# A graph network on one core: the numbers that address PSUM banks, packed four to a word and loaded every 88 steps

## The chip, the cores and the metric

The kernel runs on one NeuronCore of one Trainium2 chip. The metric is the device time of one execution in microseconds (us), lower is better. It stands at a median of 2926.83 us over three runs, from 2922.68 to 2935.74. "PE" is TensorE, "DVE" VectorE, "ACT" ScalarE, "POOL" GpSimd and "SP" SyncE. Each engine has a sequencer of its own: it reads the engine's program, keeps registers, computes addresses in them and hands matmuls on to the array. What PE's sequencer does itself is marked PEldq in the trace.

## What is computed

Four graph layers run over 3125 nodes with 512 features and 53125 edges. The edge list is sorted by the target node. Each layer adds its result to x:

```python
h = jnp.maximum(_layernorm(x, axis=-1), 0.0)
x = x + _L0_gnn_ref(h, L0_gnn_W, src, dst, edge_weight)   # relu(segment_sum(w * (h @ W)[src], dst))
h = jnp.maximum(_layernorm(x, axis=-1), 0.0)
x = x + _L1_gnn_ref(h, edge_index, L1_gnn_W, L1_gnn_b)    # sum normalised by degrees
h = jnp.maximum(_layernorm(x, axis=-1), 0.0)
x = x + _L2_gnn_ref(h, edge_index, ...)                   # sum of neighbours, two products
h = jnp.maximum(_layernorm(x, axis=-1), 0.0)
x = x + _L3_gnn_ref(h, edge_index, Ws, Wb, a_w, a_b)      # attention with 8 heads, softmax over a node's edges
```

## The kernel before

The nodes are cut into 25 tiles of 125 (`TILES`, `TN`), the sorted edges into 416 chunks of 128 (`CHUNKS`, `CE`). A chunk may hold edges of two tiles or more, so the edges are walked in `STEPS` = 416 + 25 - 1 = 440 steps; each step belongs to one tile, and which one depends on the data. DVE computes the tile of each step near the start, PE turns the four columns of it into a row in PSUM bank 3 (L1876), and DVE copies that row to `tile_row` (L757), one 32-bit number for a step.

Three stages of PE's program walk the 440 steps and need the tile's number as an address:

- **The first layer** (`step(0, i)`, from 120 us to 793 us). POOL gathers 128 rows of 2 KB for a step into a ring of 11 slots (L2258), DVE writes a selection matrix (L1104), and PE adds selection times rows into one of three PSUM banks, chosen by the tile's number (L1841, an fp32 product that runs as two passes). The sequencer does for each step: copy the number to a fresh register (L1821), wait for the selection and for the gathered rows, mask the number and add a constant (L1837, two operations), wait for the bank to be fresh, compute the bank's address (L1841, FUSED_REGOPS). Between the steps stand projections (L1807), transposes (L1796) and counts of degrees (L1883).
- **The target stage** (`target_steps`, from 2056 us to 2309 us). The last layer's scores of targets and sources are spread over the edges. PE alternates between `source_product`, six matmuls for a pair of steps (L2156), and two small matmuls, one for each step, whose moving operand `t3[:, t]` is addressed by the tile's number (L2140). For each of these the sequencer copies the number (L1821), masks it (L2140, ALU_OP) and computes the address (L2140, FUSED_REGOPS). DVE reduces each pair's result (L1432), which frees its bank (`u_sum`).
- **The last layer** (`step(LAST, i)`, from 2357 us to the end). As the first, but DVE scales the gathered rows (L1583, `scaled`), and a second small product adds the denominators (L1845) with one more address computed.

Every 20 steps `load_tiles` (L1818) loads the next 20 numbers of `tile_row` from SBUF into 20 registers (`reg_load`, TENSOR_LOAD in the trace): 22 loads in each stage, 66 in all. Another table, `group_row`, is loaded the same way 27 times between 799 and 1140 us (L1957) for other steps.

```python
def load_tiles(i):
    P.reg_load(tile_regs, tile_row[0:1, bass.ds(i, LOADED_TILES)])

def step_tile(r):
    return nc.s_assert_within(P.snap(tile_regs[r % LOADED_TILES]) & 31, 0, TILES - 1, ...)
```

The tables are announced by the semaphore `tables`, which reaches 6 when `src_t`, `dl_t`, `w_t`, `tile_row`, `end_row` and `tid_row` are written (L754 to L766). PE opens the banks then (L1890), POOL begins to gather once the last product rows are stored too, and SP reloads x.

## Time and profile before

| | |
|---|---|
| median of 3 runs | 2926.83 us (2922.68 to 2935.74) |
| profiled execution, its own time | 2952.38 us |
| its span | 2951.1 us |
| PE busy | 2508.8 us (85%) |
| DVE busy | 1854.8 us (63%) |
| POOL busy | 872.3 us (30%) |
| ACT busy | 568.5 us (19%) |
| mean granted clock of TensorE | 0.933 |

The profiled execution took 2952.38 us, 25.55 us more than the median, so differences are worked out inside it and then taken to the median. Of its own time all but 1.3 us lies in the span. A busy share is an average over stages with different limits: what a change in one stage is worth is read from that stage. "issue" as a releaser means that the engine waited for nothing that the profile can name, which for PE includes its own sequencer.

### The profile page before, as it was taken

What the parts mean: (1) busy time and instruction counts of PE and PEld (TensorE: products, weight loads), DVE (VectorE), ACT (ScalarE), POOL (GpSimd) and SP (SyncE); (2) the same over time, 40 slices, a digit from 0 to 9 for tenths busy, and PEclk for the clock granted to TensorE, in tenths of its full rate; (3) what the DMA queues carried; (4) which work ended last, traced back from release to release, by engine and by line L of the source; (5) the groups of instructions that cost most, each with busy time, mean ns of one, the idle gap of its engine ahead of it and who ended that gap; (6) DMA issues with size and microseconds to landing.
All of it is one profiled execution on the core that took longest, in us unless ns stands there. A gap on an engine that the chain in (4) does not pass through costs nothing.

```text
span 2951.1 us, 39280 instructions
## 1 busy us (share of the span) xinstructions
PE 2508.8 (85%) x10397; PEld 1450.1 (49%) x10397; DVE 1854.8 (63%) x4953; ACT 568.5 (19%) x946; POOL 872.3 (30%) x900
## 2 busy tenths in 40 slices
PE   7888988877887777999989999997898588888777
PEld 5534443433444444666555555664787433333332
DVE  7765667586588885657333443334786387776666
ACT  4533310000055553000000000001555100000000
POOL 0366666666400000000000000000002466666665
PEclk9899999898888888999999999998999699999999
DMA  6686655666422112334711121112644466676665
GB/s 164 178 241 175 181 166 167 172 168 179 117 75 86 54 54 65 94 110 112 200 43 57 57 57 54 53 32 61 152 120 138 125 193 202 204 230 189 192 189 167
DMA packets 152926, 389.06 MB, mean 132 GB/s; under 512 B 40735, under 2 KB 42136, under 8 KB 152737
## 3 DMA queue, kind: packets, MB, share of 16 engines
q0 software_dynamic: 71040, 232.25, 27.6%
q1 hardware_dynamic: 81014, 153.03, 18.4%
q8 instruction: 117, 1.92, 0.3%
q10 hardware_dynamic: 683, 1.28, 0.2%
q14 instruction: 72, 0.59, 0.1%
HBM read 333.73 MB, written 52.72 MB: 131 GB/s over the span
## 4 chain that ended last, share of the span: by engine, by line
PE 53%; DVE 23%; issue 10%; DMA 7%; another core or an unknown queue 3%; POOL 2%; ACT 1%; SPq 1%; ACTq 0%; DVEq 0%
PE banks L1841 17%; PE banks L1979 15%; PE banks L1807 7%; DVE spare L1031 4%; PE banks L2156 4%; DVE spare L1030 3%; DMA ring<-edge_counts 3%; PE banks L1971 3%; DMA ring<-table,src_t 2%; POOL ring L2313 2%; DVE sel L1104 2%; PE banks L1796 1%; DVE ring L1583 1%; DVE rstd L884 1%
## 5 line engine op out<-in xcount | busy, mean ns | idle before, releaser
L1841 PE MATMUL banks<-ring,sel 128*125 128x512 f32 x1682 | 891.4, 658 | 160.5 <-issue 116.1
L1841 PEld LDWEIGHTS banks<-ring,sel 128*125 128x125 f32 x1682 | 287.0, 199 | 476.7 <-issue 473.4
L2258 POOL DMA_INDIRECT ring<-table,src_t x440 | 436.8, 993 | 250.5 <-issue 107.7
L2292 POOL DMA_INDIRECT x<-table,src_t x25 | 25.1, 1005 | 1493.1 <-DMA x<-src_digits 1478.4
L2313 POOL DMA_INDIRECT ring<-table,src_t x401 | 386.5, 964 | 227.9 <-PE banks L1845 98.4
L1979 PE MATMUL banks<-acc,ring 125*125 125x512 f16 x1900 | 437.9, 381 | 7.0 <-issue 7.0
L1971 PE MATMUL banks<-spare 128*125 128x325 f16 x1080 | 276.0, 370 | 73.2 <-DVE spare L1031 24.2
L1979 PEld LDWEIGHTS banks<-acc,ring 125*125 125x125 f16 x1900 | 256.9, 137 | 160.4 <-issue 27.2
L1583 DVE TENSOR_TENSOR ring<-ring,banks 128x512 f32<-128x512 f32 x388 | 255.7, 682 | 122.3 <-DMA ring<-table,src_t 99.2
L1971 PEld LDWEIGHTS banks<-spare 128*125 128x125 f16 x1080 | 152.2, 147 | 197.2 <-issue 194.7
L1031 DVE TENSOR_SCALAR spare<-node_scores,flags 128x650 f16<-128x650 f16 x540 | 207.7, 385 | 0.0
L2156 PE MATMUL banks<-bias_bc,spare 123*128 123x224 bf16 x1320 | 165.3, 268 | 28.3 <-issue 15.2
L1807 PE MATMUL banks<-wh,hTh 128*125 128x512 f32 x300 | 137.0, 457 | 58.7 <-DVE hTl L900 22.4
L1030 DVE TENSOR_SCALAR spare<-node_scores,den 128x125 f16<-128x125 f16 x540 | 138.7, 257 | 62.1 <-PE banks L1971 56.8
L1432 DVE TENSOR_REDUCE big<-banks 128x16 f32<-128x448 f32 x220 | 131.4, 618 | 69.6 <-PE banks L2156 57.5
L1979 PE MATMUL banks<-acc,sel 125*125 125x512 f16 x600 | 140.6, 379 | 0.0
L1104 DVE TENSOR_SCALAR sel<-node_iota,dl_t,w_t 128x125 f32<-128x125 f32 x440 | 136.2, 358 | 1.4 <-issue 0.4
L2156 PEld LDWEIGHTS banks<-bias_bc,spare 123*128 123x128 bf16 x1320 | 119.0, 101 | 35.0 <-issue 27.0
L1807 PE MATMUL banks<-wh,hTl 128*125 128x512 f32 x300 | 126.6, 422 | 0.0
L1807 PE MATMUL banks<-wl,hTh 128*125 128x512 f32 x300 | 126.5, 422 | 0.0
L1663 ACT CAST big<-banks 125x650 f16<-125x650 f32 x125 | 90.5, 724 | 173.7 <-PE banks L1971 173.5
L1681 ACT ACTIVATE spare<-banks 125x512 f32<-125x512 f32 x25 | 14.9, 597 | 564.0 <-PE banks L1979 564.0
(408 smaller groups left out, 2970.9 us busy)
## 6 DMA issues: line engine op xcount, KB each, us to landing
ring<-edge_counts SPq DMA_DIRECT2D x38, 683.6 KB
edge_counts<-big SPq DMA_DIRECT2D x25, 683.6 KB
ring<-table,src_t POOLq DMA_INDIRECT x841
sel<-edge_counts SPq DMA_DIRECT2D x12, 683.6 KB
acc<-dst_places SPq DMA_DIRECT2D x28, 256.0 KB
x<-dst_places SPq DMA_DIRECT2D x27, 256.0 KB
acc<-src_digits SPq DMA_DIRECT2D x28, 224.0 KB
x<-src_digits SPq DMA_DIRECT2D x27, 224.0 KB
```

Source lines behind the costliest of these rows:

```text
L1030: V.tensor_scalar(out=low_hot[j % HOTS], in0=low_names, scalar1=low_t[:, j:j + 1], scalar2=None, op0=ALU.is_equal).then_inc(hot_ok, 1)
L1031: V.tensor_scalar(out=key_hot[j % HOTS], in0=key_names, scalar1=key_t[:, j:j + 1], scalar2=None, op0=ALU.is_equal).then_inc(hot_ok, 1)
L1104: V.tensor_scalar(out=sel[:, i % SELS, :], in0=node_iota[:, :], scalar1=dl_t[:, i:i + 1], scalar2=w_t[:, i:i + 1], op0=ALU.is_equal, op1=A ...
L1432: V.tensor_reduce(ue[:, pair_step(n):pair_step(n) + 2, :], bank[2 + n % 4][:, 0:2 * CTH].rearrange("p (i t h) -> p i h t", i=2, h=H), axis ...
L1583: V.tensor_tensor(slot, slot, weights[:, :, None].to_broadcast([CE, H, DP]), ALU.mult).then_inc(scaled, 1)
L1807: last = P.matmul(to, a[:, q, k, :], b[:, k, :], start=(k == 0 and n == 0), stop=(k == KB - 1 and n == 2))
L1841: last = P.matmul(to, sel[:, n % SELS, :], rows, start=False, stop=True, skip_group_check=True)
L1971: last = P.matmul(to, low_hot[j % HOTS], key_hot[j % HOTS][:, h * HALF_W:(h + 1) * HALF_W], start=False, stop=True, skip_group_check=True)
L1979: last = P.matmul(to[0:TN, :], counts_at(n, s), acc16[0:TN, s, half * D:(half + 1) * D], start=(s == half == 0), stop=(s == TILES - 1 and ...
L2156: last = P.matmul(bank[2 + n % 4][:, i * CTH:(i + 1) * CTH], sp_hot[k % 3][0:SK, j * CE:(j + 1) * CE], u3[0:SK, part, :], start=(part == 0 ...
L2258: G.indirect_dma_start(out=ring[:, i % RING, :], out_offset=None, in_=table[0][:, :], in_offset=bass.IndirectOffsetOnAxis(ap=src_t[:, i:i ...
L2313: G.indirect_dma_start(out=rows_at(i), out_offset=None, in_=table[1][:, :], in_offset=bass.IndirectOffsetOnAxis(ap=src_t[:, i:i + 1], axis ...
```

## The change

Four tile numbers of 5 bits are packed into one word. DVE makes the words by three multiplications by 32 and three additions on one partition, 110 numbers each, in place of the copy of 440. A load now fills 22 registers, which serve 88 steps, so a stage has 5 loads. A step takes its number by a shift and a mask, and one step of four (the lowest 5 bits) by the mask alone. The group table's loads stay as they were.

```diff
-    LOADED_TILES = 20
+    GROUP_STEPS = 20
+    PACKED, PACK_BITS = 4, 5
+    LOADED_WORDS = 22
+    LOADED_STEPS = PACKED * LOADED_WORDS
...
-        tile_row = sb("tile_row", [1, STEPS], I32)
+        tile_words = sb("tile_words", [1, STEPS // PACKED], I32)
+        tile_sum = sb("tile_sum", [1, STEPS // PACKED])
...
-                V.tensor_copy(tile_row[:, :], bank[3][0:1, 0:STEPS]).then_inc(tables, 1)
+                of_step = bank[3][0:1, 0:STEPS].rearrange("p (w n) -> p w n", n=PACKED)
+                for n in range(PACKED - 1, 0, -1):
+                    high = of_step[:, :, n] if n == PACKED - 1 else tile_sum[:, :]
+                    own.mark(V.tensor_scalar(out=tile_sum[:, :], in0=high, scalar1=float(1 << PACK_BITS), scalar2=None, op0=ALU.mult))
+                    V.wait_ge(v_own, own.n)
+                    own.mark(V.tensor_tensor(tile_sum[:, :], tile_sum[:, :], of_step[:, :, n - 1], ALU.add))
+                    V.wait_ge(v_own, own.n)
+                V.tensor_copy(tile_words[:, :], tile_sum[:, :]).then_inc(tables, 1)
...
-            tile_regs = [P.alloc_register(f"tile{n}") for n in range(LOADED_TILES)]
+            tile_regs = [P.alloc_register(f"tile{n}") for n in range(LOADED_WORDS)]
...
-                P.reg_load(tile_regs, tile_row[0:1, bass.ds(i, LOADED_TILES)])
-
-            def step_tile(r):
-                return nc.s_assert_within(P.snap(tile_regs[r % LOADED_TILES]) & 31, 0, TILES - 1,
+                P.reg_load(tile_regs, tile_words[0:1, i // PACKED:i // PACKED + LOADED_WORDS])
+
+            def step_tile(i):
+                word = P.snap(tile_regs[i // PACKED % LOADED_WORDS])
+                at = i % PACKED * PACK_BITS
+                return nc.s_assert_within((word >> at if at else word) & 31, 0, TILES - 1,
...
-                if i % LOADED_TILES == 0:
+                if i % LOADED_STEPS == 0:
                     load_tiles(i)
                 t = step_tile(i)
```

The condition on `LOADED_STEPS` stands in `step` and in `target_steps`. Over the whole program PE has 42 TENSOR_LOADs in place of 93 (27 of each are the group table's), 660 more REGISTER_ALUs in the two layers, and in the target stage 330 register copies have become fused register operations.

PE's program in the target stage, around a load (L1818 or, after, L1829 is the load; L2140 or L2153 the small product and its address). Register copies are not listed. Before:

```order
L2156 MATMUL banks<-bias_bc,spare 128x224 x6
L1818 TENSOR_LOAD tile_row
L2140 REGISTER_ALU
L2140 ISA
L2140 MATMUL banks<-stage,spare 128x24
L2140 REGISTER_ALU
L2140 ISA
L2140 MATMUL banks<-stage,spare 128x24
L2156 MATMUL banks<-bias_bc,spare 128x224 x6
```

And with the change:

```order
L1829 TENSOR_LOAD tile_words
L2153 REGISTER_ALU
L2153 ISA
L2153 MATMUL banks<-stage,spare 128x24
L2169 MATMUL banks<-bias_bc,spare 128x224 x6
L1832 ISA
L2153 REGISTER_ALU
L2153 ISA
L2153 MATMUL banks<-stage,spare 128x24
L1832 ISA
L2153 REGISTER_ALU
L2153 ISA
L2153 MATMUL banks<-stage,spare 128x24
```

The ISA at L1832 is the copy and the shift in one fused operation; it stands where a register copy stood (L1821), in three steps of four.

PE's program in the last layer, around a load. Before:

```order
L1818 TENSOR_LOAD tile_row
L1837 REGISTER_ALU x2
L1841 ISA
L1841 MATMUL banks<-ring,sel 125x512
L1845 ISA
L1845 MATMUL banks<-stage,sel 125x24
L1837 REGISTER_ALU x2
L1841 ISA
L1841 MATMUL banks<-ring,sel 125x512
```

And with the change:

```order
L1829 TENSOR_LOAD tile_words
L1850 REGISTER_ALU x2
L1854 ISA
L1854 MATMUL banks<-ring,sel 125x512
L1858 ISA
L1858 MATMUL banks<-stage,sel 125x24
L1850 REGISTER_ALU x3
L1854 ISA
L1854 MATMUL banks<-ring,sel 125x512
```

Here the shift is a third ALU operation. It stands behind the wait for the step's data, since that wait is held by the first of the ALU operations.

DVE's program where the tables are written, with the change (before, one CAST of 1x440 to `tile_row` stood in place of the middle seven):

```order
L760 COPY w_t<-banks 128x440
L764 TENSOR_SCALAR tile_sum<-banks 1x110
L766 TENSOR_TENSOR tile_sum<-tile_sum,banks 1x110
L764 TENSOR_SCALAR tile_sum<-tile_sum 1x110
L766 TENSOR_TENSOR tile_sum<-tile_sum,banks 1x110
L764 TENSOR_SCALAR tile_sum<-tile_sum 1x110
L766 TENSOR_TENSOR tile_sum<-tile_sum,banks 1x110
L768 CAST tile_words<-tile_sum 1x110
L769 TENSOR_SCALAR past<-acc 1x25
```

Six operations more stand ahead of `past`, `end_row` and `tid_row`, and each waits for the one before it.

## Rows read from the trace of the kernel before

**Rows 1.** The page: busy time, and the chain that ended last.
```profile
PE 2508.8 (85%) x10397; PEld 1450.1 (49%) x10397; DVE 1854.8 (63%) x4953; ACT 568.5 (19%) x946; POOL 872.3 (30%) x900
...
PE 53%; DVE 23%; issue 10%; DMA 7%; another core or an unknown queue 3%; POOL 2%; ACT 1%; SPq 1%; ACTq 0%; DVEq 0%
```

**Rows 2.** Line L1818, whole span, then 2067:2272: count, duration min/median/max in ns.
```profile
L1818 PEldq TENSOR_LOAD <-tile_row x66: 5/1360/1648, 117.8 to 2912.7; - x66
...
L1818 PEldq TENSOR_LOAD <-tile_row x21: 1355/1360/1372, 2071.1 to 2271.6; - x21
```

**Rows 3.** PE's waits, 2067:2272: waited for, us in total, times, longest.
```profile
PE banks L2140 <- issue: 16.9, 18, 1.5
PE banks L2156 <- DVE big L1432: 1.5, 4, 0.5
```

**Rows 4.** Busy time by window, 2067:2272; DVE's waits there.
```profile
2067.00:2272.00 205.00, 184.83 (x1785) 169.25 (x1781) 163.30 (x290) 125.33 (x117) 5.44 (x5) 0.96 0.49 131
...
DVE big L1432 <- PE banks L2156: 39.8, 46, 3.2
```

**Rows 5.** PE's timeline in the target stage: start, duration, operation, idle before.
```profile
2091.90 0.29 PE L2140 MATMUL banks<-stage,spare 126*128 x2
...
2095.76 0.22 PE L2140 MATMUL banks<-stage,spare 126*128 x2
...
2098.93 0.18 PE L2140 MATMUL banks<-stage,spare 126*128 x1
2100.54 0.18 PE L2140 MATMUL banks<-stage,spare 126*128 x1 [1.43 <-issue]
...
2123.60 0.20 PE L2140 MATMUL banks<-stage,spare 126*128 x2
...
2125.48 0.20 PE L2140 MATMUL banks<-stage,spare 126*128 x2
```

**Rows 6.** Sequencer operations of the target stage (L2140) and register copies (L1821).
```profile
L2140 PEldq FUSED_REGOPS  x440: 46/46/51, 2057.6 to 2308.7; - x147
L1821 PEldq MOVE  x1320: 2/29/727, 119.4 to 2940.5; - x189
```

**Rows 7.** PE's timeline in the two layers, behind a load at 387.29, 2795.62.
```profile
389.33 1.12 PE L1841 MATMUL banks<-ring,sel 128*125 128x512 f32 x2 [0.95 <-issue]
...
2797.59 0.69 PE L1841 MATMUL banks<-ring,sel 128*125 128x512 f32 x1 [0.98 <-ACT banks L1618]
```

**Rows 8.** PE's waits at L1841, 120:793 (first two) and 2345:2944.
```profile
PE banks L1841 <- issue: 53.5, 37, 4.7
...
PE banks L1841 <- DVE sel L1104: 4.3, 5, 1.3
...
PE banks L1841 <- issue: 65.9, 71, 3.9
PE banks L1841 <- DVE ring L1583: 32.2, 27, 5.0
```

**Rows 9.** POOL's waits, 120:793 and 2400:2944; its pace in the timeline.
```profile
POOL ring L2258 <- PE banks L1841: 92.0, 82, 5.4
...
POOL ring L2313 <- PE banks L1845: 78.3, 94, 2.5
...
2699.85 0.95 POOL L2313 DMA_INDIRECT ring<-table,src_t  x1 [0.30 <-issue]
2701.10 0.94 POOL L2313 DMA_INDIRECT ring<-table,src_t  x1 [0.30 <-issue]
```

**Rows 10.** Sequencer and array in the last layer: L1821, L1837, PE's timeline.
```profile
L1821 PEldq MOVE  x5: 29/29/29, 2449.8 to 2452.3; - x5
...
L1837 PEldq ALU_OP  x1760: 2/36/1397, 119.6 to 2941.5; - x196
...
2739.87 1.10 PE L1841 MATMUL banks<-ring,sel 128*125 128x512 f32 x2
...
2740.84 1.10 PE L1841 MATMUL banks<-ring,sel 128*125 128x512 f32 x2
```

**Rows 11.** DVE, POOL and PE at the tables, timeline.
```profile
107.45 0.59 DVE L757 CAST tile_row<-banks 1x440 int32<-1x440 f32 x1
...
108.25 0.17 DVE L762 TENSOR_SCALAR past<-past 1x25 int32<-1x25 int32 x1
...
113.05 0.97 POOL L2258 DMA_INDIRECT ring<-table,src_t  x1 [20.10 <-DMA table<-stage]
...
117.69 3.67 PE L1901 MATMUL banks<-ident,big 128*128 128x128 f32 x16 [6.08 <-DMA bias_bc<-in_L_gnn_b]
```

**Rows 12.** Busy time by window at the target stage's end.
```profile
2275.00:2301.00 26.00, 6.26 (x33) 3.12 (x32) 1.64 (x3) 0.00 (x0) 17.30 (x19) 0.60 0.71 201
```

More of the change, by code:

```diff
@@ L2136, in target_steps @@
                         P.wait_ge(te_sum, c - 1)
-                    if i % LOADED_TILES == 0:
+                    if i % LOADED_STEPS == 0:
                         load_tiles(i)
```

10 lines of the change are left out of this document (5 added, 5 removed).

## The prediction

> **What bounds the kernel now.** I read the page first. PE is busy 85% of the span, and the chain that ended last is 53% PE, 23% DVE and 10% "issue" [rows 1]. So PE's own pace matters in much of the program, and a part of what it loses has no other engine's name on it. The line of the loads comes next: 66 loads with a median of 1.36 us each, 22 in each of three stages [rows 2]. While the sequencer loads registers it hands on no matmul; PE then lives on what it was given before. Whether a load costs time is therefore read from PE's idle time right behind it, stage by stage.
>
> In the target stage it does. Between 2067 and 2272 us PE idles 16.9 us, 18 times, for "issue", and only 1.5 us for DVE [rows 3]; the timeline shows what this is: PE runs out of work and starts again behind a load, 1.43 us later at 2100.54 [rows 5]. DVE is busy 163.3 of these 205 us and waits 39.8 us for PE [rows 4], so PE sets the pace. More exactly, its sequencer does: between two loads a pair of steps (six matmuls and two small ones) takes (2095.76 - 2091.90) / 5 = 0.77 us, but where PE had work in store it takes (2125.48 - 2123.60) / 3 = 0.63 us [rows 5]. A sequencer at 0.77 us builds no store in which a load could hide.
>
> In the two layers it mostly doesn't. A step in the last layer takes the array 0.97 us, and the sequencer, catching up behind a load, starts a step every (2452.3 - 2449.8) / 4 = 0.63 us [rows 10], so it runs ahead and PE has a store. I went through the timeline behind each of the 44 loads: 7 in the first layer leave PE idle, 5.9 us together, and 10 in the last, 9.3 us together; one of each is shown [rows 7]. They are the loads that met PE short of data. POOL gathers at a pitch of 1.25 us and stands still for PE 92.0 us in the first layer and 78.3 us in the last [rows 9], PE in turn waits for data [rows 8]: neither holds the pace alone, and of a gain or loss on PE in these layers I count half.
>
> **The change, part by part.**
>
> *Loads of the target stage.* 17 of 22 go. At least each saves the mean idle time behind the 20 loads that end well inside the window, 16.9 / 20 = 0.84 us, so 14.4 us in all [rows 2, 3]. At most it saves its whole 1.36 us and some 0.1 us until the next operation starts, 17 x 1.46 = 24.8 us: that would be so if a store kept back by a spared load were always used later, which a 0.77 us sequencer against a 0.63 us array makes possible. I take 17 us, nearer to the lower end, because DVE becomes the next limit: its 163.3 us of work would fill 87% of 188 us [rows 4], and its bursts (scores between the reduces) already hold PE up now and then [rows 3]. What DVE has to give, 39.8 us of waiting, is more than 17.
>
> *Shifts of the target stage.* 330 register copies become fused operations. By the rows a copy lasts 29 ns and a fused operation of the same stage 46 ns [rows 6]: 330 x 17 ns = 5.6 us at most, zero at least. The fused pair does less than the address does, and it is hidden where PE has a store. I take 2 us.
>
> *Loads of the layers.* 17/22 of (5.9 + 9.3) is 11.7 us of idle time; at least nothing of it comes back, at most all. Half is 6 us.
>
> *Shifts of the layers.* 330 ALU operations are added in each layer. A step's 0.63 us on the sequencer holds five register operations and the handing on of matmuls [rows 10], so one more costs about 0.1 us. Against 0.97 us of array time 0.73 us is still hidden, and these 66 us of sequencer time cost nothing as long as PE has a store: that is their cover. Without a store the shift is in the path, since it stands behind the wait for the step's data. PE ran dry at L1841 37 + 5 + 71 + 27 = 140 times [rows 8]. Three steps of four carry a shift: 140 x 3/4 x 0.1 = 10.5 us at most, zero at least. Half is 5 us. Behind the waiting ALU operation stand only the same step's products; who waits for those are POOL (slot), DVE (selection) and ACT (finished tile).
>
> *Packing on DVE.* Six dependent operations on one partition are added and a cast shrinks from 0.59 us. Operations of 25 numbers take 0.17 us at a pitch of 0.20 [rows 11]; for 110 numbers, some read from PSUM, I bound them at 0.2 to 0.35 us, net 0.8 to 1.8 us. They delay `tables`, now complete by about 108.7 us. I cost this at nothing: POOL doesn't gather before 113.05, when the last product rows have landed, and PE doesn't go on before 117.69, when a bias has landed [rows 11]. Without that cover it would cost up to 1.8 us. SP passes the same wait only after issuing that bias.
>
> *Five loads that stay* fill 22 registers in place of 20: the median hardly moves. They fall at steps 0, 88, 176, 264 and 352.
>
> Sum: -17 + 2 - 6 + 5 = -16 us. The profiled execution would go from 2952.4 to 2936, the median from 2926.8 to 2911. That the profiled one is 25.6 us over the median is no term: it has a stretch of 26 us in which PE was busy 6.3 us and every engine but POOL crawled [rows 12], and a new profile may have it or not.
>
> What the timeline shows for an ALU operation is 36 ns [rows 10], not the 0.1 us between starts. The Trainium skill (Perfetto Trace Analysis, Per-instruction lifecycle) says that of a sequencer-only instruction the profiler reports the execution alone, and neither fetch and decode nor the wait. By the 36 ns the shifts of the layers would be 140 x 3/4 x 0.036 = 3.8 us at most, and the sum -18 us with half of that; by that rule, with which the 0.63 us per step agree, it is the larger price that counts.
>
> **The rivals.**
>
> *A: the sequencer is freed wholly.* Each spared load gives 1.46 us in the target stage, the idle time of the layers comes back in full, shifts cost 2: -24.8 + 2 - 11.7 + 5 = -30, so 2897 us. For it speaks the 0.77 against 0.63 us per pair; against it DVE's 80% share and POOL's pitch of 1.25 us, which no PE shortens. Chance 0.17.
>
> *B: the gain is absorbed.* In the target stage DVE's reduces (0.54 us apart at best) and its bursts make PE wait in place of the load, so that only half of 14.4 us comes through, and the layers, held by gathers, give nothing: -7 + 2 - 0 + 3 = -2 to -7, say 2922 us. For it speaks that DVE has but 42 us to spare and that its waits would fall on PE in four bursts; against it that DVE waits 46 times and PE only 4. Chance 0.27.
>
> *C: slower, by the shift behind the wait.* In the layers each shift lengthens the way from the landed data through PE to the freed slot and back to POOL. If the ring of 11 slots makes this the pace at most steps, each shift costs 0.1 us: 660 x 0.1 = 66 us, and the sum is 2926.8 - 17 + 2 - 6 + 66 = 2972 us. The kernel is no faster once the share x of shifts in the path passes 21 / 66 = 0.32, and slower by over 0.5% beyond 36 / 66 = 0.54. By the rows x is at most 105 / 660 = 0.16. For it speaks that POOL waits for PE in 176 of its gathers [rows 9]; against it the dense stretches at 0.97 us. Chance 0.06.
>
> *D:* that the loads don't go is excluded by the order of instructions: 15 stand where 66 stood.
>
> **How the numbers follow.** Half a per cent, 14.6 us, is about what a measurement of this kernel can tell from no change. The forecast has 0.50, A 0.17, B 0.27, C 0.06. The forecast's own range is 2903 to 2918; 2912.2 is the bound for "faster", so of its 0.50 some 0.33 fall below and 0.17 above it. With A this gives faster 0.50. B and the rest of the forecast give 0.44, and C splits into 0.01 there and 0.05 slower; together: faster 0.50, same 0.45, slower 0.05. The range takes in A from below and B from above, with the 3 us by which medians of a few runs differ: 2894 to 2928. Outside are C and the ends of A and B.
>
> **What would show it.** Right: 15 loads at L1829, each still 1.36 us; PE's "issue" waits in the target stage down from 17 us to some 3 to 5; the stage (first load to the last before 420 steps are done, 2056.0 to 2271.6) shorter by some 15 us; pairs still 0.77 us apart where no load stands. DVE's waits for PE fall by about as much, and PE's for DVE grow a little. In the layers PE's idle time at L1841 stays within 10 us and the lengths within 5. Wrong: pairs that slow to 0.85 us or more, since then the fused shift has its price; waits of PE for L1432 over 10 us (B); layers longer by over 10 us with POOL waiting more for PE (C); or a target stage shorter by 25 us (A).

## The result, and the profile after

The changed kernel is slower: 2956.79 us (median of 4 runs, 2942.13 to 2963.60) against 2927.82 us of the kernel before on the same chip (4 runs), ratio 1.0073 with a 95% interval of 1.0050 to 1.0097. Three later comparisons, on chips 4, 5 and 15, gave 1.0059, 1.0039 and 1.0030, all intervals above 1. The sign is settled; by the ratios the size is 9 to 21 us (the two medians above are 29 us apart, the ratio of 1.0073 stands for 21 us, 15 to 28). One execution of after_again (3476.62 us) and one of the kernel before in the fifth set (4632.22 us) were far slower than the rest and are left out of ratios, medians and clocks.

The execution profiled of the change took 2942.13 us, that of before 2952.38 us. So the two profiles stand in the other order than the medians: the profile shown of before was a long one of its kind. What follows compares stages, not spans. The page of the change, busy time and chain that ended last, against [rows 1]:

```profile
PE 2515.3 (86%) x10397; PEld 1452.2 (49%) x10397; DVE 1856.3 (63%) x4959; ACT 567.8 (19%) x946; POOL 871.2 (30%) x900
...
PE 54%; DVE 22%; issue 10%; DMA 5%; another core or an unknown queue 4%; POOL 2%; ACT 1%; ACTq 0%; SPq 0%; DVEq 0%
```

Nothing moved between engines. The line of the loads comes next, against [rows 2]: the whole line, then the loads at steps 0, 88, 176 and 264 of the target stage, one by one (duration min/median/max in ns, start in us):

```profile
L1829 PEldq TENSOR_LOAD <-tile_words x15: 1254/1857/5258, 116.3 to 2804.1; - x15
...
L1829 PEldq TENSOR_LOAD <-tile_words x1: 1848/1848/1848, 2054.9 to 2054.9; - x1
L1829 PEldq TENSOR_LOAD <-tile_words x1: 5212/5212/5212, 2097.6 to 2097.6; - x1
L1829 PEldq TENSOR_LOAD <-tile_words x1: 1857/1857/1857, 2141.6 to 2141.6; - x1
L1829 PEldq TENSOR_LOAD <-tile_words x1: 5217/5217/5217, 2185.8 to 2185.8; - x1
```

The loads are 15, as they should be, but not one of the four lasts 1.36 us. Two extra words bring a load to 1.85 us, and every second one takes 5.2 us. Step 88 is word 22, byte 88 of the table, and 88 is not a multiple of 16; step 176 is word 44, byte 176, which is. All starts of L1818 in the kernel before (multiples of 80 bytes) were multiples of 16.

PE's and DVE's waits in the target stage (waited for: us in total, times, longest), against [rows 3, 4], and PE's busy time in the same window:

```profile
PE banks L2153 <- issue: 12.2, 7, 5.2
PE banks L2169 <- DVE big L1443: 2.7, 5, 0.8
...
DVE big L1443 <- PE banks L2169: 36.8, 56, 5.6
...
2067.00:2272.00 205.00, 188.09 (x1806) 169.77 (x1803) 163.83 (x289) 124.18 (x116) 7.92 (x8) 0.96 0.49 133
```

18 short stops became 7, but their sum fell only from 16.9 us to 12.2. PE's timeline shows a regular stretch and the load behind it:

```profile
2084.60 0.25 PE L2153 MATMUL banks<-stage,spare 126*128 x2
...
2097.03 0.29 PE L2153 MATMUL banks<-stage,spare 126*128 x2
...
2097.84 0.18 PE L2153 MATMUL banks<-stage,spare 126*128 x1
2103.18 0.20 PE L2153 MATMUL banks<-stage,spare 126*128 x1 [5.16 <-issue]
2103.31 1.28 PE L2169 MATMUL banks<-bias_bc,spare 123*128 123x224 bf16 x6
```

One load left PE idle for 5.16 us, and the matmuls behind it ran at about half speed (six in 1.28 us against 0.73): the trace's granted clock is 0.5 from 2101.59 to 2108.41 us and 1.0 on both sides. Between loads, 15 pairs of steps took 2097.03 - 2084.60 = 12.43 us, 0.83 us each, not 0.77. Over the first 200 pairs of the stage the median distance is 0.81 us in the change and 0.77 in the kernel before. The register operations say why (L1832 was L1821, against [rows 6]):

```profile
L1832 PEldq MOVE  x990: 2/29/754, 118.4 to 2929.8; - x198
L1832 PEldq FUSED_REGOPS  x330: 57/62/73, 2057.1 to 2304.6; - x165
```

A copy fused with the shift lasts 62 ns, 33 more than the copy alone; the fused operation of before that I priced it from lasts 46.

The packing on DVE cost nothing, as costed. Its timeline:

```profile
106.47 0.25 DVE L764 TENSOR_SCALAR tile_sum<-banks 1x110 f32<-1x110 f32 x1
106.75 0.26 DVE L766 TENSOR_TENSOR tile_sum<-tile_sum,banks 1x110 f32<-1x110 f32 x1
...
108.11 0.21 DVE L768 CAST tile_words<-tile_sum 1x110 int32<-1x110 f32 x1
```

From 106.47 to 108.32 for what a cast of 0.59 us did before, so 1.3 us net. POOL's first gather began at 111.96 and PE went on at 116.24 behind the same bias transfer as before.

The two layers are not quieter (PE's waits, 120:793, then 2345:2944, against [rows 8]):

```profile
PE banks L1854 <- issue: 67.8, 55, 5.2
...
PE banks L1854 <- DVE sel L1115: 9.7, 5, 4.7
...
PE banks L1854 <- issue: 77.5, 56, 4.1
PE banks L1854 <- DVE ring L1594: 15.5, 12, 4.1
```

"Issue" grew from 53.5 + 65.9 = 119.4 us to 67.8 + 77.5 = 145.3 us, although 34 loads had gone from these stages. Behind the ten that stay PE idles 10.5 us, behind the 44 before it was 15.2 us. So the growth is not right behind the loads and needs another explanation.

**A second kind of chip.** The experiments ran on five chips, numbered 3, 4, 5, 6 and 15; the number of the result's chip isn't known, and it may be one of these. Chips 3 and 6 ran the kernel before in 2742 us, chips 4, 5 and 15 in 2930 to 2955, and the result's chip in 2928. The rows of both kinds are worth reading. First an ALU operation at L1837 and a copy on SP's queue (L2546), then PE's queue between 137 and 158 us (L1821), each in the kernel before, on the slower kind of chip (the profile from which the prediction was made):

```profile
L1837 PEldq ALU_OP  x1760: 2/36/1397, 119.6 to 2941.5; - x196
...
L2546 SPq MOVE out<-x x25: 3/29/709, 2602.0 to 2948.7; - x25
...
L1821 PEldq MOVE  x11: 4/16/714, 137.2 to 157.9; - x11
L1837 PEldq ALU_OP  x21: 3/660/731, 136.5 to 157.2; - x21
```

and in the same kernel on chip 3:

```profile
L1837 PEldq ALU_OP  x1760: 32/36/42, 119.2 to 2731.7; - x196
...
L2546 SPq MOVE out<-x x25: 29/29/37, 2438.0 to 2739.2; - x25
...
L1821 PEldq MOVE  x14: 29/29/29, 139.0 to 157.0; - x14
L1837 PEldq ALU_OP  x28: 36/36/36, 138.6 to 156.6; - x28
```

The medians over the whole program are equal (36 ns); only the maxima and the window differ. On the slower kind, stretches of up to 31 us come up again and again in which many register operations take 0.7 us, on PE's queue and on SP's. They lie in the two layers, where POOL issues gathers; the stages between have none. ACT's queue has none either: in no run does one of its 375 register operations last over 44 ns. The packets of the gathers' DMA queue took equally long on both kinds, a median of 159 ns. A window of such a stretch, on the slower kind and on chip 3 (PE busy, PEld, DVE, ACT, POOL, granted clock, DMA share, GB/s):

```profile
128.00:158.00 30.00, 17.24 (x28) 5.62 (x28) 28.93 (x73) 22.03 (x61) 20.90 (x20) 0.81 0.94 269
```
```profile
128.00:158.00 30.00, 24.05 (x44) 7.21 (x43) 28.99 (x73) 21.31 (x60) 23.03 (x23) 0.89 1.01 286
```

PE ran 28 matmuls there against 44 in the same 30 us. The 26 us at the end of the target stage [rows 12], which I took for an accident of one execution, are of the same kind: there the operations last as long as elsewhere, but weight loads and matmuls follow each other 0.7 us apart (starts at 2277.71, 2278.42, 2279.14 us), while POOL issues the first gathers of the last layer. From the product of step 418 to the first product of the last layer it takes 75 to 88 us in every profile of the slower kind, and 43 to 49 on chips 3 and 6. I call these crawling stretches. They were in the profile before I predicted, in the maxima of [rows 6] and [rows 10], and I read past them: 727 ns beside a median of 29.

### The profile page after: what moved, and what is told of

It reads as the page before. It is cut to its first block, busy times and chain, and to the rows that moved or that the text cites. A ratio compares the mean times of both kernels' runs of the same rounds, so it can differ in the third digit from the quotient of the medians.

```text
span 2940.8 us, 39895 instructions
## 1 busy us (share of the span) xinstructions
PE 2515.3 (86%) x10397; PEld 1452.2 (49%) x10397; DVE 1856.3 (63%) x4959; ACT 567.8 (19%) x946; POOL 871.2 (30%) x900
## 3 DMA queue, kind: packets, MB, share of 16 engines
q10 hardware_dynamic: 683, 1.28, 0.2%
## 4 chain that ended last, share of the span: by engine, by line
PE 54%; DVE 22%; issue 10%; DMA 5%; another core or an unknown queue 4%; POOL 2%; ACT 1%; ACTq 0%; SPq 0%; DVEq 0%
PE banks L1854 17%; PE banks L1992 15%; PE banks L1818 6%; PE banks L2169 5%; DVE spare L1042 3%; PE banks L1984 3%; DVE spare L1041 3%; DMA ring<-edge_counts 3%; DVE sel L1115 2%; POOL ring L2326 2%; DMA ring<-table,src_t 2%; PE banks L1807 1%; DVE stage L865 1%; PE banks L2072 1%
## 5 line engine op out<-in xcount | busy, mean ns | idle before, releaser
L1818 PE MATMUL banks<-wh,hTh 128*125 128x512 f32 x300 | 135.7, 452 | 50.7 <-DVE hTl L911 14.5
L1858 PEld LDWEIGHTS banks<-stage,sel 128*125 128x125 bf16 x440 | 64.3, 146 | 125.6 <-issue 125.6
L1818 PE MATMUL banks<-wh,hTl 128*125 128x512 f32 x300 | 124.8, 416 | 0.0
L1818 PE MATMUL banks<-wl,hTh 128*125 128x512 f32 x300 | 124.6, 415 | 0.0
```

What stands on the lines that cost most here:

```text
L1818: last = P.matmul(to, a[:, q, k, :], b[:, k, :], start=(k == 0 and n == 0), stop=(k == KB - 1 and n == 2))
```

## The experiments

Theories. **A**: the loads that stay are long (5.2 us where they don't begin at a multiple of 16 bytes), the shifts of the target stage are in the path, and a register operation added to the layers costs little, except on chips with crawling stretches, where it has its share of the 0.7 us operations. **C**: what costs is that the shift stands behind the wait for a step's data, the cause that rival C of the prediction named; the other letters have nothing to do with the prediction's rivals. **B** and **E**: the change costs what it costs on every chip, crawling or not. Differences in us are the ratio less 1, times the median of before on that chip; intervals are 95%. The expectations of the first two sets were written before the crawling stretches were understood, and each says in its own words what it tests, under letters of its own.

### First set: the parts on one chip (chip 4, before 2929.79 us)

**after_again**, the changed kernel once more.

> The changed kernel once more, unaltered, in five rounds, to see whether its 2942 to 2964 us stands against a before of 2923 to 2936. If the slowdown belongs to the kernel (long loads or shifts), its median is 1.005 to 1.010 of before again and its TensorE clock is 0.914 to 0.925 against 0.933. If it was a matter of the chip or of the hour, the ratio falls within 0.5% of 1. In the trace, the loads at steps 88 and 264 of each stage last 5.2 us again and the other three 1.85 us.

Measured: 2945.11 us, ratio 1.0059 [1.0036, 1.0082], +17 us. The slowdown repeats, as expected for a cost of the kernel, and so do the loads: 5.21 to 5.24 us at steps 88 and 264 of each stage.

**packed20**: the change with loads of 20 words, each from a multiple of 80 bytes.

```diff
-    LOADED_WORDS = 22
+    LOADED_WORDS = 20
+    WORDS = -(-STEPS // PACKED // LOADED_WORDS) * LOADED_WORDS
...
-        tile_words = sb("tile_words", [1, STEPS // PACKED], I32)
+        tile_words = sb("tile_words", [1, WORDS], I32)
```

> Packed words as in the change, but loaded 20 at a time every 80 steps, from a table padded to 120 words, so that each load starts at a multiple of 80 bytes. Theory L (loads): a load costs 0.27 us for each aligned piece of 16 bytes and 0.24 us for each word that is not part of one, so all 18 loads last 1.36 us, none 5.2; the stalls of 4 to 5 us on PE go and with them the fall of the clock. Then the kernel comes to 15 us under before, some 2912 us, and 40 us under the change. Theory S (shifts): the 330 shifts of each stage are what costs, whatever the loads last; then it stays within 10 us of the change, near 2950 us.

Measured: 2936.6 us, ratio 1.0021 [1.0007, 1.0034], +6 us. The load line, five loads of the target stage, and PE's waits there:

```profile
L1831 PEldq TENSOR_LOAD <-tile_words x5: 1356/1362/1371, 2087.9 to 2241.3; - x5
...
PE banks L2155 <- issue: 6.7, 10, 1.5
```

Three loads more than the change, of 1.36 us by the median, and 11 us less. So the long loads cost about that much. They are not all: theory L had expected 2912 us, 40 under the change, and even with every load aligned the kernel stays 6 us slower than before. Theory S, within 10 us of the change, isn't excluded by the time alone; the stage is 9.5 us shorter than with the change (198.9 against 208.4 us), which S had not.

**shifts_alone**: 66 loads as before, numbers stored 32 times larger in three steps of four, and shifted back.

```diff
-                return nc.s_assert_within(P.snap(tile_regs[r % LOADED_TILES]) & 31, 0, TILES - 1,
+                word = P.snap(tile_regs[i % LOADED_TILES])
+                return nc.s_assert_within((word >> 5 if i % 4 else word) & 31, 0, TILES - 1,
```

> The kernel before with its 66 loads of 20 unpacked numbers, but the numbers of three steps in four are stored times 32 and shifted back, so that PE's sequencer has the change's shifts and nothing else of it. Theory S: 25 to 50 us slower than before, since the gain of fewer loads is missing too; pairs of the target stage go from 0.77 to 0.85 us or the layers grow by over 10 us each. Theory L: within 10 us of before, at most 7 us for the shifts that I costed (2 + 5).

Measured: 2950.43 us, ratio 1.0080 [1.0057, 1.0104], +23 us. My prediction had 7 us for all 990 shifts. So theory L's 10 us fall, and theory S's lower bound of 25 lies inside the interval (17 to 30). The change has the same shifts and 51 loads fewer, and is only 6 us better than this; packed20 is 17 us better.

**loads22**: nothing packed or shifted, 22 numbers a load every 22 steps.

```diff
-    LOADED_TILES = 20
+    LOADED_TILES = 22
+    GROUP_STEPS = 20
```

> The kernel before, unpacked and without shifts, but with 22 numbers for a load and a load every 22 steps: 20 loads in a stage, every second of which starts 8 bytes off a multiple of 16. Theory L: those last 5.2 us and the others 1.85 us, 30 x 5.2 + 30 x 1.85 = 212 us of loading in place of 66 x 1.36 = 90 us; in the target stage, where the sequencer sets the pace, 10 x 3.8 + 10 x 0.5 - 2 x 1.36 = 40 us come on top, in the layers a part, so 50 to 100 us slower than before. Theory S: no shift is added, the times of the loads don't matter, within 15 us of before.

Measured: 2983.39 us, ratio 1.0183 [1.0162, 1.0203], +54 us, with six loads fewer than before. The line as a whole, the first two loads of the target stage (bytes 0 and 88 of the stage's table), and PE's waits there:

```profile
L1819 PEldq TENSOR_LOAD <-tile_row x60: 433/3716/6141, 116.2 to 2944.5; - x60
...
L1819 PEldq TENSOR_LOAD <-tile_row x1: 1851/1851/1851, 2058.0 to 2058.0; - x1
L1819 PEldq TENSOR_LOAD <-tile_row x1: 5233/5233/5233, 2073.1 to 2073.1; - x1
...
PE banks L2141 <- issue: 52.1, 23, 5.2
```

That is inside theory L's 50 to 100 us and far outside S's 15; the target stage, 255.5 us from its first matmul to the product of step 418 against 210.8, is longer by 45 us where L had 40. So it is not the packing: 22 words from a multiple of 16 bytes take 1.85 us, 22 from 8 bytes off it take 5.2. The three durations fit (an estimate from these rows) 1.36 / 5 = 0.27 us for each piece of 16 bytes and some 0.24 us for each single word, if a load that starts off a multiple of 16 takes all its words singly: 5 pieces and 2 words are 1.85, 22 single words 5.2. The Trainium skill (Runtime: NRT & Kernel Launch, Instruction fetch mechanics) gives about 200 ns a register for a register load, in bulk too; the loads it describes come from HBM, these from SBUF. The 5.2 / 22 = 0.24 us of the unaligned load are near that; the 1.36 / 20 = 0.07 us of the aligned one are not, and there the measurement decides.

The same was to be read in the trace of the kernel before, on another engine. ACT loads 5 numbers of a table (`group_end`, L1656) 25 times, from bytes 0, 20, 40 and so on; every fourth start, 7 in all, is a multiple of 16 bytes. Those seven loads last 0.54 to 0.55 us, the other 18 last 2.35 to 2.42. All 25, then the first and the second of them:

```profile
L1656 ACTq TENSOR_LOAD <-stage x25: 541/2377/2424, 798.6 to 1139.7; - x25
...
L1656 ACTq TENSOR_LOAD <-stage x1: 554/554/554, 798.6 to 798.6; - x1
L1656 ACTq TENSOR_LOAD <-stage x1: 2357/2357/2357, 817.6 to 817.6; - x1
```

Off the multiple this is 2.4 / 5 = 0.48 us a word, so the estimate of 0.24 holds for PE's loads only. Some of PE's aligned loads of the group table, too, lasted up to 2.9 us in the trace of before in place of 1.36, which stays unexplained.

### Second set: the shifts, stage by stage (chip 3, before 2742.48 us)

**before_again**, the kernel before, for a profile on this chip.

> The kernel before, unaltered, for a second trace: its first one took 2952 us, over every timed run of it (2924 to 2940). If the lengths of the stages in the first trace were typical, the two traces agree within 3 us in each stage; I rather expect that the first one lies some 20 us high, in stretches that have nothing to do with loads, so that it hid the price of the shifts. Ratio 1.000, within 0.2%.

Measured: 2741.67 us, ratio 0.9997 [0.9985, 1.0009]. Its profile is the one of chip 3 shown above. The chip was another than that of the first trace, so it can't say whether that trace was a long one in stretches of its own, as I had suspected.

**shifts_target** and **shifts_layers**: all numbers stored times 33, so that they can be read with or without a shift; one kernel shifts in the target stage alone, the other in the two layers alone.

```diff
-                V.tensor_copy(tile_row[:, :], bank[3][0:1, 0:STEPS]).then_inc(tables, 1)
+                V.tensor_scalar(out=tile_row[:, :], in0=bank[3][0:1, 0:STEPS], scalar1=33.0, scalar2=None, op0=ALU.mult).then_inc(tables, 1)
...
+                return nc.s_assert_within((word >> 5 if shifted and i % 4 else word) & 31, 0, TILES - 1,
```

> The kernel before with a shift in three of four steps of the target stage alone: the table holds each number twice in one word (n * 33), so that it reads the same with and without a shift. Both stages together cost 21 us. Theory T (target stage): the sequencer sets its pace, so fused copy-and-shift operations that last longer than a copy cost 330 times their difference: 10 to 18 us slower than before, and the stage 10 us longer or more. Theory W (shift behind the wait): 0 to 5 us, since the fused operation stands ahead of no wait there.

> The kernel before with the shifts in the two gather layers alone, 660 more ALU operations behind the wait for the step's data. Theory W: 15 to 20 us slower than before, which is 660 x 0.1 us times a share in the path of 0.25 to 0.3, in place of my 0.08. Theory T: 2 to 8 us.

Measured: shifts_target 2750.34 us, ratio 1.0026 [1.0015, 1.0038], +7 us; shifts_layers 2742.51 us, ratio 1.0007 [0.9994, 1.0021], +2 us. Together 9 us, where shifts_alone had cost 23 on chip 4. The target stage's +7 lies between the two theories (T 10 to 18, W 0 to 5), the layers' +2 at T's lower bound and far from W's 15 to 20.

**packed20_early2**: packed20, and in the layers the shift and the mask are done ahead of the waits, in registers of their own.

```diff
+                if at:
+                    P.reg_alu(high_reg, word, at, ALU.logical_shift_right)
+                P.reg_alu(now_reg, high_reg if at else word, 31, ALU.bitwise_and)
...
-                t = step_tile(i)
+                t = early_tile(i)
```

> The packed table with aligned loads of 20 words, and in the two layers the shift and the mask are done ahead of the waits for data, into a register of their own; behind the wait one ALU operation and the address are left, one operation fewer than the kernel before has there. The sequencer executes as many operations as with the change. Theory W: what counts is what stands behind the wait, so this gains 15 to 25 us on the packed table without it (2937 us) and comes to 2912 to 2922 us, under before. Theory C (count): the number of operations per step is what costs, wherever they stand: within 5 us of 2937 us.

Measured: 2734.12 us, ratio 0.9970 [0.9954, 0.9986], 8 us faster than before. Its expected times were for the chip of the first set. From this run it can't be said whether the early shift or the chip did it; hence the third set.

### Third set: ahead of the wait or behind it (chip 5, before 2933.66 us)

**after_third**, the changed kernel.

> The changed kernel once more, beside the three below. Theory A (each register operation that is added in the gather layers costs almost nothing while PE's sequencer keeps its 0.1 us pitch, and about 0.7 us in the stretches where single register operations last 0.7 us): where the profile shows no register operation of PE over 0.45 us (as on the chip of before_again), the change is within 6 us of the kernel before (its loads give 8 us in the target stage, its shifts cost 9); where it shows 200 or more of them, 15 to 30 us slower. Theory B (the change costs its 20 us or so by its long loads and shifts whatever the chip): 15 us or more slower on every chip.

Measured: 2942.38 us, ratio 1.0039 [1.0017, 1.0060], +11 us, with 317 register operations of PE's queue that last 0.45 us or more (counted in the trace among copies, ALU and fused operations; the kernel before has 233). Less than the 15 expected, with an interval that holds it.

**early_third**, packed20_early2 again.

> Packed numbers in loads of 20 words from multiples of 16 bytes, shift and mask done ahead of the waits in the two layers. Theory A: the shifts still stand in the sequencer's row, so on a chip with 0.7 us register operations it wins only by the loads: within 8 us of the kernel before; on a chip without them 5 to 12 us faster. Theory C (what cost the time was that the shift stands behind the wait, on the way from a gather's arrival to its product): 10 us or more faster on either chip.

Measured: 2934.47 us, ratio 1.0009 [0.9993, 1.0025], +3 us: within A's bound, and not C's 10 us faster. The same kernel was 8 us faster than before on chip 3.

**before_early**: the kernel before with mask and copy ahead of the waits, nothing shifted.

```diff
+                P.reg_alu(now_reg, tile_regs[i % LOADED_TILES], 31, ALU.bitwise_and)
...
-                t = step_tile(i)
+                t = early_tile(i)
```

> The kernel before with nothing packed and nothing shifted; in the two layers the mask of the tile's number and its copy are done ahead of the waits (as many register operations as before, one or two fewer behind each wait). Theory C: 5 us or more faster than the kernel before. Theory A: within 4 us of it on either chip, since the number of operations in the sequencer's row is unchanged.

Measured: 2933.33 us, ratio 1.0002 [0.9984, 1.0020]. C falls: what stands behind the wait and what stands ahead of it cost the same.

**ops_added**: two unused shifts more ahead of each step of the layers.

```diff
+                for _ in range(2):
+                    P.reg_alu(spare_reg, tile_regs[i % LOADED_TILES], 1, ALU.logical_shift_right)
```

> The kernel before with two register shifts more ahead of each step of the two layers, their result unused (1760 operations; the change added 660). Theory A: on a chip whose profile shows register operations of 0.7 us, about one in 30 of the added ones lasts so: 1760/30 x 0.65 = 38 us slower (20 to 60). On a chip without them the layers' products hide them: within 8 us. Theory C (only what stands behind the waits costs): within 8 us on either chip.

Measured: 2933.12 us, ratio 0.9997 [0.9979, 1.0016]. This run priced nothing. Its instructions are those of the kernel before: the compiler removed operations whose result nobody used, as the count of register operations in the trace shows (7980 in both). It is worth as much as a second run of the kernel before, no more.

### Fourth set: the shifts on a chip that crawls (chip 15, before 2955.03 us)

**ops_live**: the same idea with a result that is used. Numbers are stored times 1057, and two shifts by five bits stand ahead of the waits; the compiler makes one fused operation of them, so 880 operations are added.

```diff
+                P.reg_alu(ones_reg, tile_regs[i % LOADED_TILES], 5, ALU.logical_shift_right)
+                P.reg_alu(twos_reg, ones_reg, 5, ALU.logical_shift_right)
+                P.reg_alu(now_reg, twos_reg, 31, ALU.bitwise_and)
```

> The kernel before, its table in numbers of 1057 times the tile, and in the two layers two shifts by five bits ahead of the waits of every step, on which the tile's number depends (the compiler makes one fused operation of the two: 880 operations more on PE's sequencer). Theory A (on a chip whose sequencers have stretches of 0.7 us an operation, each added operation has its share there): 15 to 25 us slower where the profile shows such stretches, within 4 us where it does not. Theory E (register operations are covered there too and it is the target stage and the loads that cost): within 5 us on either chip.

Measured: 2973.09 us, ratio 1.0047 [1.0029, 1.0065], +14 us (9 to 19). E's 5 us are outside the interval; A's 15 to 25 are narrowly missed by the median and held by the interval. before_early, at +1 us on chip 5, differs from it only by these shifts and the factor in the table. So operations ahead of every wait do cost time on such a chip.

**shifts_layers_b** and **shifts_target_b**, the two kernels of the second set.

> The shifts in the two layers alone (660 operations), as in shifts_layers, perhaps on another chip. Theory A: 12 to 18 us slower where the profile shows register operations of 0.7 us; 0 to 4 where it does not, as on the chip of shifts_layers. Theory E: within 5 us on either.

> The shifts in the target stage alone (330, in one fused operation with the copy). No gather of POOL runs there, and the profiles show no register operation of 0.7 us in this stage on any chip, so both theories expect 5 to 8 us slower, as the stage of shifts_alone was 5 us longer and that of shifts_target 7. Theory E would need 15 us or more on a chip of the slow kind to make up the 20 of shifts_alone.

Measured: shifts_layers_b 2967.29 us, ratio 1.0033 [1.0018, 1.0049], +10 us (5 to 15), against +2 us (-2 to 6) on chip 3. shifts_target_b 2965.40 us, ratio 1.0027 [1.0015, 1.0038], +8 us, against +7 us on chip 3. The target stage costs the same on both kinds of chip; the layers cost more where the queue crawls. The step is somewhat smaller than the 12 us I had expected at least, and the two intervals of the layers touch, so its direction is better supported than its size.

**after_fourth**, the changed kernel.

> The changed kernel once more. Theory A: within 6 us of the kernel before where the profile shows no register operation of 0.7 us; 8 to 20 us slower where it shows them. Theory E: 10 to 20 us slower on either.

Measured: 2964.60 us, ratio 1.0030 [1.0013, 1.0047], +9 us (4 to 14): within A's 8 to 20, and by the interval within E's 10 to 20 too. The changed kernel itself was not run on chip 3 or 6, where A has it level with the kernel before within 6 us.

What the traces of all runs count, as register operations of PE's queue that last 0.45 us or more (each some 0.7 us):

```
chips that crawl, nothing added in the layers
                   before 233, loads22 234 (chip 4), before_early 233 and ops_added 227
                   (chip 5), shifts_target_b 225 (chip 15)
660 or 880 operations added in the layers
                   after 328
                   chip 4   after_again 272, packed20 304, shifts_alone 310
                   chip 5   after_third 317, early_third 303
                   chip 15  after_fourth 314, shifts_layers_b 279, ops_live 278 (880 added)
chips 3 and 6      before_again, shifts_target, shifts_layers, packed20_early2,
                   packed_target, packed20_b: none
```

660 operations added in the layers brought 38 to 95 slow ones more. For shifts_layers_b it is 279 - 225 = 54, or 54 x 0.7 = 38 us of queue time, of which about 10 us came out at the end. The shift in the target stage, which has no crawling stretch where it was counted, brought none.

### Fifth set: the change without its two costs (chip 6, before 2742.44 us)

**packed_target**: the layers load and mask as in the kernel before. In the target stage alone four numbers a word are read, in 6 loads of 20 words from multiples of 80 bytes; they lie in the upper bits of the first 110 words of the same table.

```diff
+                V.tensor_tensor(tile_row[:, 0:WORDS], tile_row[:, 0:WORDS], whole, ALU.bitwise_or).then_inc(tables, 1)
...
-                    if i % LOADED_TILES == 0:
-                        load_tiles(i)
-                    t = step_tile(i)
+                    if i % (PACKED * LOADED_TILES) == 0:
+                        load_tiles(i // PACKED)
+                    word = P.snap(tile_regs[i // PACKED % LOADED_TILES])
+                    t = nc.s_assert_within((word >> (i % PACKED + 1) * PACK_BITS) & 31, 0, TILES - 1,
```

> The two layers as in the kernel before (44 loads of 20 words, no shift); in the target stage alone four numbers a word, in the upper bits of the first 110 words of the same table, 6 loads of 20 words from multiples of 16 bytes in place of 22, and a shift in all 440 steps, fused with the copy. Theory A with the stage lengths so far (packed20 took 199 us for the target stage, the kernel before 211): target stage 196 to 203 us, the layers unchanged, 6 to 12 us faster than the kernel before on either kind of chip. Theory E (every shift costs, hidden or not, and the loads give little): within 4 us of the kernel before, or slower.

**packed20_b**: packed20 beside it.

> Packed numbers in the layers too, in loads of 20 words from multiples of 16 bytes (packed20 once more, beside packed_target on the same chip). Theory A: where the profile shows register operations of 0.7 us, 10 to 16 us slower than packed_target, by its 660 shifts in the layers (shifts_layers_b cost 12); where it shows none, within 4 us of packed_target. Theory E: level with packed_target on either.

Measured: packed_target 2732.49 us, ratio 0.9962 [0.9950, 0.9973], 10 us faster than before; packed20_b 2733.59 us, ratio 0.9964 [0.9947, 0.9982], 10 us faster. PE's waits in the target stage (1985:2190), before_again (chip 3) and packed_target (chip 6):

```profile
PE banks L2140 <- issue: 17.8, 18, 1.4
PE banks L2156 <- DVE big L1432: 2.8, 5, 1.4
```
```profile
PE banks L2155 <- issue: 5.5, 8, 1.6
PE banks L2171 <- DVE big L1445: 3.7, 5, 1.4
```

This is close to the picture that I had predicted for the change, "issue" from 17 us to 3 to 5, and the stage took 200.3 us, within the expected 196 to 203. The gain is 8 to 10 us and not 15, since the shifts of the stage take their part. E fell with it, in what it said of packed_target. Chip 6 doesn't crawl, so the two kernels are level, as A expects there (and E everywhere); that packed_target keeps its 10 us on a chip that crawls is argued from the parts (its layers are those of before) and not shown: it wasn't run there.

The stage lengths, worked out from the traces (start of a stage's first matmul to that of its last; target: of its first small product to that of step 418), put the parts together, in us:

```
chips that crawl   before  after  shifts_alone  packed20  shifts_target_b  before_early  after_third
chip                    -      -             4         4               15             5            5
first layer         676.8  671.3         672.5     670.2            684.7         666.5        672.1
target              210.8  208.4         216.0     198.9            217.2         210.2        208.3
last layer          587.4  586.3         582.3     582.4            586.9         582.4        582.9

no crawl     before_again  shifts_target  packed_target  packed20_b
chip                    3              3              6           6
first layer         580.7          581.2          585.5       580.3
target              208.7          215.7          200.3       199.1
last layer          519.0          516.0          512.0       515.7
```

The target stage repeats within 1 or 2 us; single profiles of the layers differ by 5 to 10 us, and by chip, so for them the medians of the runs count and not this table. In the target stage all shifts cost 5 to 7 us, the loads of the change give back 8, and aligned loads of 20 words 17.

A last pair shows where the time of the layers goes. The last layer's window (before_early, after_third; columns as above):

```profile
2341.00:2923.00 582.00, 482.59 (x1354) 205.09 (x1354) 425.63 (x904) 35.93 (x93) 375.84 (x390) 0.95 0.69 198
```
```profile
2341.00:2924.00 583.00, 494.80 (x1354) 213.67 (x1355) 425.11 (x905) 36.39 (x93) 376.60 (x390) 0.91 0.68 198
```

The same 1354 matmuls take 12 us more, at a mean granted clock of 0.91 in place of 0.95: 109 us of this window were granted 1.2 GHz, against 59 us, as those behind the 5.16 us stop were. Over all executions the mean clock of the kernel before was 0.931 on chips 4 and 5 and 0.928 on chip 15, that of the change 0.923, 0.922 and 0.919. It isn't the long loads alone: on chip 4 shifts_alone had 0.923 and packed20 0.924, neither with a long load, while on chips 3 and 6 every kernel had 0.956 to 0.959. On a chip that crawls a queue that stops PE for longer costs the stop and then some of the speed behind it. These two profiles took the same time in this stage, so this pair shows a shift in what fills it and no loss.

## Why the prediction was wrong

Forecast 2911 us (2894 to 2928), measured 2956.79; the chance given to "slower" was 0.05. Two steps failed: the shifts, priced at 7 us, and the five loads that stay, priced as if they were the old ones. On chip 4, where the parts ran side by side, the forecast of -16 us became +17, 33 us off. Of these 16 are the shifts (shifts_alone +23 in place of +7), 11 the long loads (after_again against packed20), and 6 the gain of the layers' loads, of which nothing was seen. So aligned loads alone would not have saved the forecast: with them the change is 6 us slower on chip 4 and 10 us faster on chip 6, and in neither place 16 us faster. Point by point:

- **"Five loads that stay fill 22 registers in place of 20: the median hardly moves."** This step failed outright. The loads that stay last 1.85 us or 5.2 us, by the byte at which they begin. Fifteen of them hold the queue for 48 us in the trace of the change, against 87 us for the 66 in that of before, not the 20 that 15 x 1.36 would be. I counted what the change took away and gave its new instruction the duration of the old one, though its address had changed. All 66 loads that I had looked at start at multiples of 16 bytes, but the same trace holds ACT's loads at L1656, 0.55 us or 2.4 us by their start; I did not look there, and did not bound this term from both sides as I did the rest.
- **Loads of the target stage, -17 us.** The term was right for aligned loads: target stage 216.0 to 198.9 us from shifts_alone to packed20, and "issue" down to 6.7 us. The change itself got 8 of it (216.0 to 208.4).
- **Shifts of the target stage, +2 us (0 to 5.6).** Mis-sized: measured +7 and +8 on two chips, one of each kind. The fused copy and shift lasts 62 ns, not 46, and the pair of steps grew from 0.77 to 0.81 us by the median. The queue sets the pace here, as I had said, so the shifts were in the path, and my own argument called for the upper end; and the upper end was itself too low, since 330 x 33 ns is 10.9 us and not 5.6. The pair stayed under the 0.85 us that I had named as the mark of this failure.
- **Loads of the layers, -6 us.** Not measured alone. shifts_alone to packed20 gave 17 us in all on chip 4, as much as the target stage alone became shorter, which leaves nothing clear for the layers.
- **Shifts of the layers, +5 us (0 to 10.5), by 140 dry moments.** +2 us on chip 3, where the step holds; +10 (5 to 15) on chip 15, at the upper end; on chip 4 the shifts of both kinds of stage were not run apart, and 23 - 7 = 16 us would be left for the layers. The step that failed is the cover: PE's store, which was to hide an operation of 0.1 us, is gone in a crawling stretch, where many operations take 0.7 us: PE's waits for "issue" at the layers' products, 42.4 + 66.6 us in before_early, are 60.1 + 76.1 us in after_third on the same chip. The rate that I used was the median's, and the cost sat in the maxima.
- **Packing, 0.** Right: 1.3 us more on DVE, and nobody waited.
- **"A new profile may have it or not"** of the crawl at the end of the target stage: wrong. Every profile of the slower kind has it, and none on chips 3 and 6.
- **Rival C** gave the right sign, by the wrong mechanism: with nothing shifted, ahead of the wait or behind it makes no difference (before_early), and ops_live, with its shifts ahead of the wait, is slower all the same. That the sign was right is luck.

With the measured parts the sum for a crawling chip is: target stage, shifts +7 and loads -8; layers, shifts +10; the loads of the layers unknown. That is +9, the value of after_fourth on chip 15, where the shifts of the two kinds of stage were measured. On the other chips +11, +17 and +21 were measured, and the 8 to 12 us over that are open. On chip 4 some 6 us of them need no long load: shifts_alone is 6 us over its two parts (+7 and +10), and packed20 6 us over its sum of 0, though the intervals are as wide as that. Candidates are a dearer shift on some chips (310 slow operations on chip 4 against 279 on chip 15), with the lower clock that comes with it, and the 5.2 us loads in the layers (PE idles 1.0 to 4.1 us behind each of the four).

## What to carry to other kernels

When a change makes an operation rarer but larger, price the new one by its own size and start, look in the trace for one of its kind on any engine (ACT's loads at L1656 showed 0.55 us and 2.4 us), and when its address was aligned before by luck, keep it so. Read the maximum beside the median in a line of small queue operations: 727 beside 29 ns says that there are stretches in which an operation that you add may cost over twenty times its price. Here 38 to 95 of 660 did. And on a queue that sets the pace, an added operation belongs into the sum at its full length.

## What the runs showed of the hardware

- On PE's queue a register load of 20 words from a multiple of 16 bytes took 1.36 us by the median, of 22 words 1.85 us, and of 22 words from 8 bytes off such a multiple 5.2 us. On ACT's queue a load of 5 words took 0.55 us from a multiple of 16 bytes and 2.4 us from others.
- A register copy took 29 ns, fused with a shift 62 ns.
- Chips 4, 5 and 15 and the chip of the result showed stretches in which many register operations on PE's and SP's queues took 0.7 us while POOL issued gathers (225 to 234 of PE's 7980 in kernels with nothing added), and ran the kernel before in 2928 to 2955 us; chips 3 and 6 showed none and ran it in 2742 us. Why is open. ACT's queue showed none on either kind. In the kernel before the first layer took 677 us on one kind and 581 on the other, the last 587 and 519; the stages between, from the first layer's end to the target stage, took 1261 us on both.
